# Value products and six projection tiles as 64-row matmuls side by side, with the scores issued unit by unit

## The reference

```python
b, n, m = 4, 77, 1024            # context rows, tokens
h, d = 16, 64                    # heads
xn = layernorm(context); ln = layernorm(layernorm(x))
q = ln @ Wq                                        # 256 -> 16 * 64
kv = concat([xn @ Wkv, ln @ Wkv], axis=1)          # 77 + 1024 keys
sim = einsum('bhid,bhjd->bhij', rmsnorm(q, qn_g) / 8, rmsnorm(k, kn_g))
out = einsum('bhij,bhjd->bhid', softmax(sim), v)
x = x + out @ Wout + bout
x = x + shared_ffn(layernorm(x)) + top_2_of_8_experts(layernorm(x))
```

## Time and profile before

| | |
|---|---|
| median of three runs | 2591.28 us |
| profiled execution | 2582.26 us |
| its span (first to last instruction) | 2580.4 us |
| busy, share of the span: PE, its weight loads, DVE, ACT, POOL | 96%, 74%, 67%, 65%, 49% |
| mean granted clock of PE, as a share of 2.4 GHz | 0.984 |

### The profile page before, as it was taken

How to read it: one execution, slowest core, us unless ns; L and a number is a source line. 1 busy time by engine, 2 the same in 40 slices (tenths; PEclk the granted TensorE clock), 3 DMA queues, 4 the chain that set the end, 5 groups by cost and what they waited for, 6 DMA issues and landing times. The chain is left out here.

```text
span 2580.4 us, 46535 instructions
## 1 busy us (share of the span) xinstructions
PE 2469.2 (96%) x15720; PEld 1899.8 (74%) x15720; DVE 1737.1 (67%) x2516; ACT 1677.3 (65%) x2286; POOL 1275.5 (49%) x783
## 2 busy tenths in 40 slices
PE   3799999999999999999999999997989999999997
PEld 3566666666666666666666666656989999999997
DVE  7666766666667666676666666765876557767675
ACT  2577877787778777787788777883333344454443
POOL 4445434453455445543455344522534526666665
PEclk8899999999999999999999999998989999999999
DMA  5423422233223322332223322246822459999996
GB/s 182 155 81 92 129 87 76 84 121 104 82 78 125 103 78 86 99 121 86 78 88 122 97 82 78 86 124 128 175 84 77 141 185 318 326 317 319 323 323 170
DMA packets 231441, 361.76 MB, mean 140 GB/s; under 512 B 59559, under 2 KB 139739, under 8 KB 227400
## 3 DMA queue, kind: packets, MB, share of 16 engines
q1 hardware_dynamic: 204694, 301.66, 38.0%
q0 software_dynamic: 25696, 58.82, 8.2%
q10 hardware_dynamic: 978, 0.34, 0.1%
HBM read 280.90 MB, written 79.85 MB: 140 GB/s over the span
## 5 line engine op out<-in xcount | busy, mean ns | idle before, releaser
L826 ACT ACTIVATE pr_hi<-ps_s 128x1024 fp32r<-128x1024 f32 x512 | 524.6, 1025 | 262.0 <-PE ps_s L948 260.7
L717 DVE TENSOR_TENSOR pr_lo<-ps_s,pr_hi 128x1024 fp32r<-128x1024 f32 x288 | 351.8, 1221 | 257.1 <-ACT ps_s L827 256.9
L962 PE MATMUL ps_o<-pr_hi,vA 128*65 128x512 f32 x1152 | 472.4, 410 | 1.4 <-DVE o_first L646 0.8
L717 DVE TENSOR_TENSOR pr_lo<-pr,pr_hi 128x1024 fp32r<-128x1024 f32 x288 | 354.3, 1230 | 163.7 <-ACT pr L827 163.7
L964 PE MATMUL ps_o<-pr_lo,vA 128*65 128x512 f32 x1152 | 454.0, 394 | 0.0
L963 PE MATMUL ps_o<-pr_hi,vC 128*65 128x512 f32 x1152 | 452.9, 393 | 0.0
L455 POOL TENSOR_TENSOR sq<-raw 128x1024 f32<-128x1024 f32 (+1 forms) x96 | 134.1, 1397 | 625.3 <-ACT raw L771 625.3
L1613 ACT ACTIVATE ht<-f_ps_h,b 128x256 f32<-128x256 f32 x440 | 184.5, 471 | 339.6 <-PE f_ps_h L1545 306.4
L1545 PE MATMUL f_ps_h<-xT_hi,w 128*128 128x256 f32 x1760 | 355.1, 285 | 2.4 <-DVE xT_lo L1647 2.3
L917 PE MATMUL ps_m<-w_sb,lnT_sb 128*128 128x384 f32 (+1 forms) x1728 | 349.2, 341 | 4.2 <-DVE q_lo L659 2.5
L917 PEld LDWEIGHTS ps_m<-w_sb,lnT_sb 128*128 128x128 f32 x1728 | 298.2, 191 | 59.7 <-issue 36.4
(11 more groups left out here) (214 smaller groups left out, 4394.9 us busy)
## 6 DMA issues: line engine op xcount, KB each, us to landing
w<-w1S_dram SPq DMA_DIRECT2D x160, 512.0 KB, 6.3
lnT_sb<-lnT_dram SPq DMA_DIRECT2D x31, 2304.0 KB, 9.0
w2raw<-in_L_ffn_Wproj SPq DMA_DIRECT2D x78, 512.0 KB, 6.4
w1S_dram<-cut POOLq DMA_DIRECT2D x36, 512.0 KB, 3.0
rec<-rden_dram SPq DMA_DIRECT2D x63, 256.0 KB, 3.7
routed_dram<-empty POOLq DMA_DIRECT2D x28, 387.0 KB, 3.6
xt<-routed_dram SPq DMA_DIRECT2D x39, 258.0 KB
w_raw<-in_L_xattn_Wkv SPq DMA_DIRECT2D x66, 128.0 KB, 3.7
```

What stands on the lines that cost most here:

```text
L717: v.tensor_tensor(pr_lo[:, ring(w, d), :], full_of(d), pr_hi[:, ring(w, d), :].bitcast(F32), ALU.subtract).then_inc(s_lo, 1)
L826: act.activation(pr_hi[:, ring(w, d), :], ps_s[:, d % 2, :], ACT.Exp, bias=bias)
L962: mm(out, upper, pr_hi[:, r, cols], start=k == 0, stop=False)
```

## The change

All of it is in the attention.

- **Values in halves.** `values_half` contracts over 64 of the 128 keys of a unit. A pair of matmuls takes rows 0 to 63 for one head and rows 64 to 127 for the other; which head has which rows is `swap`, the parity of d. A unit is done in two parts of three pairs: part 0 at d = unit + 2 (`first`), part 1 with the halves swapped at d = unit + 3 (`second`). Only the very last unit of the last window uses the old form. Part 1 waits until part 0 is complete (`s_half`).
- **Projections in halves.** Tiles (1, 2), (5, 6) and (7, 8) are projected as pairs of 64-row matmuls in the same way, at d = 8, 13 and 15 (`project_halves`), part 0 ahead of `second` and part 1 behind it. Tile 0 (at d = 6) and tiles 3 and 4 (at d = 11) keep all rows, as do the transposes, now at d = 2, 4 and 6.
- **Order.** PE takes one unit at a time: scores, jobs, `second`, `first`. At d = 2 and 11 the jobs stand between `second` and `first`.
- **Who frees the score banks.** The full exponential goes to `pr` for five units (0, 1, 9, 16, 17) and into `ps_s` for the other thirteen.
- **DVE's list.** `output` is one copy of both heads, at the same places; `squares` moves to d = 14, 17 and 2, `divide` of the second group to d = 9, the two steps on `vA` and `vC` to d = 3 and 5.

```diff
@@ -75,8 +75,11 @@
 MOST = 70.0
 PARTS = (("k", 0, 4), ("q", 0, 4), ("k", 4, 8), ("q", 4, 8), ("k", 8, 9))
 TURNS = len(PARTS)
-FIRST_TURN = 2
-FIRST_PROJ = FIRST_TURN + TURNS
+TURNED = {2: (0, 1), 4: (2, 3), 6: (4,)}
+PROJECTED = {6: (0,), 8: (1, 2), 11: (3, 4), 13: (5, 6), 15: (7, 8)}
+HALVED = (8, 13, 15)
+BETWEEN = (2, 11)
+SPARED = (0, 1, 9, 16, 17)
...
         def full_of(d):
 
-            return pr[:, 0, :] if d % 2 else ps_s[:, 0, :]
+            return pr[:, d % 2, :] if d in SPARED else ps_s[:, d % 2, :]
...
             def output(w, h, before):
 
                 wait(dve, s_store[h], w.n(16, -16 * before))
-                wait(dve, s_pv0, w.n(2, h + 1 - 2 * before))
-                v.tensor_copy(o_sb[h][0:DH + 1, 0:512], ps_o[0:DH + 1, 0, :]).then_inc(s_o, 1)
                 wait(dve, s_pv, w.n(UNITS, KT * (h + 1) - UNITS * before))
-                v.tensor_copy(o_sb[h][0:DH + 1, 512:N], ps_o[0:DH + 1, 1, :]).then_inc(s_o, 1)
+                v.tensor_copy(o_sb[h][0:DH + 1, :].rearrange("p (r n) -> p r n", r=2), ps_o[0:DH + 1, :, :]).then_inc(s_o, 1)
...
                         if w.attend and not w.first:
-                            if d == 3:
+                            if d == 5:
                                 invert(w, 1, 1)
-                            if d == 7:
+                            if d == 9:
                                 divide(w, 1, 1)
-                        if w.attend and d == 12:
+                        if w.attend and d == 13:
                             invert(w, 0, 0)
                         if w.attend and d == 16:
                             divide(w, 0, 0)
-                        if w.turn and FIRST_TURN <= d < FIRST_TURN + TURNS:
-                            turned(w, d - FIRST_TURN)
-                        if w.turn and d in (2, 4):
-                            values(w, d == 4)
-                        if w.proj and d in (11, 15):
-                            squares(w, (d - 11) // 4)
+                        if w.turn:
+                            for i in TURNED.get(d, ()):
+                                turned(w, i)
+                        if w.turn and d in (3, 5):
+                            values(w, d == 5)
+                        if w.proj and d in (14, 17):
+                            squares(w, (d - 14) // 3)
                         if closing(w) and w.s == 1 and d in (4, 6, 9, 11):
                             lower(d)
-                        if d == 0 and not (isinstance(w.v, int) and (w.v == -1 or 2 * w.v + w.s == WINDOWS - 1)):
+                        if d == 2 and not (isinstance(w.v, int) and (w.v == -1 or 2 * w.v + w.s == WINDOWS - 1)):
                             squares(w, 2 - GROUPS)
...
-                        if d % 2:
+                        if d in SPARED:
                             wait(act, s_lo, w.n(UNITS, d - 1))
...
+            products = [(a, b, c) for a, b in ((0, 0), (0, 1), (1, 0)) for c in range(C)]
+
+            def project(w, tile):
+                ready(w, tile)
+                out, lo = ps_m[:, tile % 2, :], 0 if tile < NT else PW
+                for k, (a, b, c) in enumerate(products):
                     ins = mm(out[:, lo:3 * PW], lnT_sb[:, a, c, tile * P:(tile + 1) * P], w_sb[:, w.slot, b, c, lo:],
                              start=k == 0, stop=k == 3 * C - 1)
                 ins.then_inc(s_job, 1)
+
+            def project_halves(w, n, tiles, part):
+                for k, (a, b, c) in enumerate(products):
+                    for j, tile in enumerate(tiles):
+                        if part == 0 and k == 0:
+                            ready(w, tile)
+                        if part == 1 and k == 0 and j == 0:
+                            pe.wait_ge(s_jobhalf, w.n(len(HALVED), 2 * len(HALVED) + n + 1))
+                        rows = slice(DH * (j ^ part), DH * (j ^ part) + DH)
+                        lo, last = 0 if tile < NT else PW, part == 1 and k == 3 * C - 1
+                        ins = mm(ps_m[:, tile % 2, lo:3 * PW], lnT_sb[rows, a, c, tile * P:(tile + 1) * P],
+                                 w_sb[rows, w.slot, b, c, lo:], start=part == 0 and k == 0, stop=last)
+                        if last:
+                            ins.then_inc(s_job, 1)
+                if part == 0:
+                    ins.then_inc(s_jobhalf, 1)
...
-            def values(w, d):
+            def weights(w, d):
 
                 slot, d_ = (w.slot, d) if d >= 0 else (w.other, d + UNITS)
                 g, k, r = d_ // KT, d_ % KT, ring(w, d)
+                return g, k, [(v_[:, slot, k, :, 0:DH + 1], p_[:, r, :]) for v_, p_ in ((vA, pr_hi), (vC, pr_hi), (vA, pr_lo))]
+
+            def begin(w, d, g, k):
+
                 pe.wait_ge(s_lo, w.n(UNITS, d + 1))
+                if k == 0:
+                    wait(pe, s_o, w.n(2, g))
+
+            def values(w, d):
+
+                g, k, pairs = weights(w, d)
+                begin(w, d, g, k)
                 for h in range(2):
-                    if k == 0:
-                        wait(pe, s_o, w.n(4, 2 * g + h - 1))
-                    upper, lower = vA[:, slot, k, h, 0:DH + 1], vC[:, slot, k, h, 0:DH + 1]
-                    cols, out, last = slice(512 * h, 512 * h + 512), ps_o[0:DH + 1, h, :], k == KT - 1
-                    mm(out, upper, pr_hi[:, r, cols], start=k == 0, stop=False)
-                    mm(out, lower, pr_hi[:, r, cols], start=False, stop=False)
-                    ins = mm(out, upper, pr_lo[:, r, cols], start=False, stop=last)
-                    if last and h == 0:
-                        ins.then_inc(s_pv0, 1)
+                    for i, (v_, p_) in enumerate(pairs):
+                        ins = mm(ps_o[0:DH + 1, h, :], v_[:, h], p_[:, 512 * h:512 * h + 512],
+                                 start=k == 0 and i == 0, stop=k == KT - 1 and i == 2)
                 ins.then_inc(s_pv, 1)
+
+            def values_half(w, d, part, swap):
+
+                g, k, pairs = weights(w, d)
+                if part == 0:
+                    begin(w, d, g, k)
+                else:
+                    pe.wait_ge(s_half, w.n(UNITS, d + 1))
+                for i, (v_, p_) in enumerate(pairs):
+                    for t in range(2):
+                        h, rows = t ^ swap, slice(DH * t, DH * t + DH)
+                        ins = mm(ps_o[0:DH + 1, h, :], v_[rows, h], p_[rows, 512 * h:512 * h + 512],
+                                 start=k == 0 and part == 0 and i == 0, stop=k == KT - 1 and part == 1 and i == 2)
+                ins.then_inc(s_pv if part else s_half, 1)
...
+                    def second(d):
+                        if w.attend and not (w.first and d < LAG + 1):
+                            values_half(w, d - LAG - 1, 1, d % 2)
+
+                    def first(d):
                         if w.attend and not (w.first and d < LAG):
                             if d == LAG:
                                 pe.wait_ge(s_v, w.n(2, 2))
-                            values(w, d - LAG)
-
-                    for d in range(0, UNITS, 2):
+                            if last and d == UNITS - 1:
+                                values(w, d - LAG)
+                            else:
+                                values_half(w, d - LAG, 0, d % 2)
+
...
-                            wait(pe, s_lo, w.n(UNITS, d - 1))
+                            wait(pe, s_exp if (d - 2) % UNITS in SPARED else s_lo, w.n(UNITS, d - 1))
                             scores(w, d, general)
-                            if general and (d + 1) % KT == 0:
-                                maximum(w, (d + 1) // KT)
-                            wait(pe, s_exp, w.n(UNITS, d))
-                            scores(w, d + 1, general)
-                        if d - LAG == KT - 1:
-                            weigh(d)
-                            job(d)
-                            job(d + 1)
-                            weigh(d + 1)
+                        if w.proj and d in HALVED:
+                            project_halves(w, HALVED.index(d), PROJECTED[d], 0)
+                            second(d)
+                            project_halves(w, HALVED.index(d), PROJECTED[d], 1)
+                            first(d)
+                        elif d in BETWEEN:
+                            second(d)
+                            jobs(d)
+                            first(d)
                         else:
-                            job(d)
-                            weigh(d)
-                            job(d + 1)
-                            weigh(d + 1)
+                            jobs(d)
+                            second(d)
+                            first(d)
```

More of the change, by code:

```diff
@@ L222, in attention @@
         s_scores, s_exp, s_lo, s_pv = t.sem("a_scores"), t.sem("a_exp"), t.sem("a_lo"), t.sem("a_pv")
-        s_pv0, s_o = t.sem("a_pv0"), t.sem("a_o")
+        s_o, s_half, s_jobhalf = t.sem("a_o"), t.sem("a_half"), t.sem("a_jobhalf")
```

(46 more changed lines are left out.)

2 lines of the change are left out of this document (added).

## The result

The changed kernel takes 2601.6 us (median of 6 runs, 2599.2 to 2605.6), the kernel before 2589.6 (6 runs beside it): ratio 1.0049, 95% interval 1.0036 to 1.0062. It is slower by 0.5%. Forecast were 2612 us, a range of 2532 to 2640, and 0.52 for slower.

A forecast was written before the change was run, and what follows sets the result against it. PE was taken to set the pace. Window borders +9, first and last windows -4 and clock +17 gave 2604 us; the runs' median lies 9.0 higher, 2613, stated as 2612, range 2532 to 2640 (its own 2597 to 2635).

The forecast's parts named there:

- Trips: On PE, going out of 64-row form and back costs 0.4 us; five trips fewer a window save 2.0 us.
- The own sum: PE's work in one window of the attention, waits left aside: 50.1 us, against a period of 52.23 before.
- the bare end of the copy: At `first` of d = 2, 0.35 us of waiting for the `ps_o` copy that the transposes do not cover.
- tile 8's share: Projection tile 8, 256 columns riding beside tile 7 on PE, costs 0.3 us more a window than before.
- rival 4: Projection pairs load weights one behind the other, 0.214 us replacing 0.177 at 384 columns: 2639 us, chance 0.09.
- The chain: DVE, ACT and POOL work from unit 14's scores to `first` of d = 2: 19.5 us, against PE's 17.1.
- units 16 and 17 and the divide between them come one after another behind `nrm`: DVE's two subtractions and divide wait for POOL's `nrm`, then take 3 x 1.14 = 3.4 us, ahead of `sq`.
- one gap of 2.4 us: PE waits 2.4 us at `first` of d = 2 for the late copy, making the window 52.5 us.
- The clock: Thin PE stretches at d = 2 bring half clock in four windows of ten: 12 x 1.4 = 17 us.
- rival 1: The wait at `first` of d = 2 is there but the clock stays: 2596 us, chance 0.17.
- Rival 2: DVE is on time for the copy and the change does what the trips promise: 2535 us, chance 0.18.
- rival 3: POOL does not hold DVE up, the wait is 1.1 us less, 51.4 a window: 2562 us, chance 0.11.

The follow-up runs named there:

- e4: Also run 4: the changed kernel with `squares` of group 0 at d = 12 and a prefetch hint on PE's loop-end branch; 2516.7 us, ratio 0.9736.
- e7: e4 with the scores of unit 3 put ahead of `first` of d = 2, behind the transposes; 2512.4 us, ratio 0.9720.
- e11: Also run 11: e4 with all nine projection tiles as full-row matmuls; 2545.5 us, ratio 0.9849.
- run 1: The changed kernel with `squares` of group 0 at d = 12 instead of 14, no hint; 2549.4 us, ratio 0.9863.
- run 8: The changed kernel with the branch hint and unit 16's full exponential kept in PSUM instead of SBUF; 2567.4 us, ratio 0.9931.
- Run 9: The changed kernel with the branch hint and the first group's divide at d = 15 instead of 16; 2559.7 us, ratio 0.9906.
- run 10: run 1 with all projection tiles full-row and the PE loop's first instruction at the start of a 16 KB code block; 2546.1 us, ratio 0.9853.
- run 3: The changed kernel with only a prefetch hint for the branch that closes PE's loop; 2592.4 us, ratio 1.0026.
- run 12: The kernel before with the prefetch hint on PE's loop-end branch; 2585.6 us, ratio 1.0005.
- run 6: The kernel before with 16 unused semaphore increments behind each unit's scores in PE's loop; 3012 us, ratio 1.1658.

## Why the prediction came out right, and where it was wrong

Its time was right to 10 us, its direction too, but only some of its steps hold, and that the sum came so near is in part luck.

- **Trips, right.** The own sum was 50.1 and 50.5 with the bare end of the copy; e4, where only that end is left, has 50.2, and e7, which covers it, 50.1. Three trips less tile 8's share were put at 3 x 0.4 - 0.3 = 0.9; e11 gives 1.0. Projection pairs start every 0.177 us in the changed kernel, not every 0.214, so rival 4 and its weight loads are out.
- **The chain, right in length, wrong in order.** I counted 19.5 us from the scores of unit 14 to `first` of d = 2; they start at 980.51 and 999.81, 19.3. The mechanism, POOL and DVE keeping each other from SBUF, is shown by runs 1 and 8: take the overlap or one of the two SBUF operands away, and the long subtraction is gone (2.69 us becomes 1.23). The step that failed is "units 16 and 17 and the divide between them come one after another behind `nrm`": `sq` got in behind unit 16 and not behind unit 17, so the gap stands one slot earlier and 1.66 us long, with 0.46 at the copy. In the kernel of run 8 `sq` came behind both, as written, and the gap at the copy was 1.3 to 1.8 us, not 2.4. What decides who comes first was not settled.
- **A whole loss missed.** The prediction has no word on the code. It costs 2.1 to 2.7 us from start to start at each of 13 jumps, and since it hides the other gap there, its removal alone is worth only about 5 us and some 33 once the chain is short (run 4 against run 1). That the forecast was near all the same is this hiding, and luck: it had one gap of 2.4 us at each of 30 borders, and the kernel has gaps of about that size in sum at nearly each (52.3 and 52.9 us a window for the 52.5 forecast), from two causes in turn.
- **The clock, the mis-sized term.** I took twelve half-clock stretches of 1.4 us, 17 in all. There are four (clock 0.57 to 0.74 in their windows of 4 us); their windows take 54.1 to 54.6 instead of 52.9 us, so about 6 us together, all behind the jump and none behind DVE's wait of 1.66. Nor does the term come out in the kernel of run 8, which has the gap that it was made for: four stretches there too. The length of the stall does not settle it: 1.81 us was followed by half clock once, 2.29 three times not:

```profile
1149.00:1153.00 4.00, 2.17 (x10) 1.53 (x12) 4.00 (x3) 0.80 (x2) 2.57 (x1) 0.74 0.02 4
...
1574.00:1578.00 4.00, 3.78 (x20) 2.48 (x22) 4.00 (x3) 1.94 (x2) 1.19 (x1) 0.57 0.05 12
```

  The 11 us between this term and the measured one are the forecast's error: 2612 - 11 = 2601. So rival 1 (the clock stays, 2596) was nearer than the forecast.
- **Rivals 2 and 3.** DVE on time came about only with run 1's edit, and then part of the gain, some 33 of 80 us, was kept back by the code. Rival 2 asked for "2 us less anywhere in the chain". Run 9 took 1.1 out and gained 1.1 a window; from its 51.4 to e4's 50.2 another 1.2 would be needed, so 2.3 in all by this estimate, and no run takes out just 2. That 51.4 is also rival 3's number, but not its mechanism: POOL still held DVE up there.

## What to carry over

Count the instructions of a loop's body when a change splits instructions in two: the code line of the page (packets before and after) and gaps marked "issue" behind the jump show it, and a hint on the branch (runs 4 and 11) or the head's place in memory (run 10) can mend it. Where two waits meet at one place, removing either alone shows little, so test both together before you call one worthless (5 and 48 us alone, 80 together). In this chain across engines the edit at the head gave most: with the code out of the way, one `squares` moved by two units gave 76 us (run 4 against run 3), the divide moved by one 33, the operand 25.

## What the chip showed unexpectedly

- Code: a PE loop body of 1239 instructions was fetched once and stayed; 1667 and 1817 were fetched anew in each turn, nine packets of 16 KB. With the branch hinted, 1817 stayed too (47 packets), and 1667 did with its head on a block (45). The Trainium skill, Runtime: NRT & Kernel Launch (Instruction fetch mechanics), gives PE 128 KiB in blocks of 16 KiB, 2048 instructions, and says that a taken branch to a block outside the two current ones forces a fetch and stalls. The traces agree on the stall where there is a fetch: 1.7 to 2.3 us in the changed kernel, 2.0 to 3.2 with the store and the load running beside it. They do not agree on the two blocks: the body of 1239, some five blocks, jumps back without a fetch. Nor does size alone decide: both 1667 and 1817 stayed in one run and were fetched anew in another, and what rule of prefetch lies behind that was not settled.
- The hint did nothing where the code stayed anyway (run 12).
- In run 6 an increment of a semaphore by an instruction of its own holds PE's sequencer for 0.151 us, where the 36 loads and matmuls of a unit issue in 2.07, 0.06 each: such an increment is dearer to it than a matmul.
- Matmuls of two row groups do not keep in step. Tile 8's 256 columns let its row group run ahead, and value matmuls of `second` start singly while matmuls of tile 7 that stand ahead of them in the program have yet to start (at d = 13, with two tiles of 384 columns, they start in pairs). So the last matmul in the program is not the last to be done: `s_jobhalf` goes up with tile 8's last one of part 0, which starts at 931.11, and tile 7 has two more of part 0, at 931.24 and 931.42. Part 1 starts at 931.92, behind `second`, and that keeps the parts apart here; the semaphore alone does not say that tile 7 is through with part 0:

```profile
931.24 0.52 PE L938 MATMUL ps_m<-w_sb,lnT_sb 64*128 64x384 f32 x2
931.46 0.39 PE L1008 MATMUL ps_o<-pr_hi,vC 64*65 64x512 f32 x1
931.60 0.39 PE L1008 MATMUL ps_o<-pr_hi,vA 64*65 64x512 f32 x1
```
